# Layer-norm statistics of a transformer layer: three Newton steps from a bit-trick guess on VectorE, or a power on GpSimd and one Newton step

## The reference

```python
def _layernorm(x, eps=1e-05):
    m = jnp.mean(x, axis=-1, keepdims=True)
    v = jnp.var(x, axis=-1, keepdims=True)
    return (x - m) / jnp.sqrt(v + eps)

# attention, 16 heads of 16 features
q, k = features(split(x @ Wq + bq)), features(split(x @ Wk + bk))
#   features(y) = exp(y - max(y)) / (sum(exp(y - max(y))) + 1e-6)
probs = einsum('bhld,bhmd->bhlm', q, k) / (sum(q) + 1e-6)
x = _layernorm(x + merge(probs @ v) @ Wo + bo)

# feed-forward network, every operand through fp4_quant_dequant
#   scale = max(|block of 16|) / 6; round x / scale to a grid of 8 magnitudes
h = silu(fp4_linear(x, w_gate)) * fp4_linear(x, w_up)     # width 704
x = _layernorm(x + fp4_linear(h, w_down))
```

## Time and profile before

| what | value |
|---|---|
| time, median of 3 runs | 815.86 us (815.85 to 816.23) |
| time of the profiled execution | 815.38 us |
| its span | 813.6 us |
| TensorE busy | 734.0 us (90%) |
| VectorE busy | 747.7 us (92%) |
| ScalarE busy | 580.8 us (71%) |
| GpSimd busy | 573.3 us (70%) |
| mean granted TensorE clock | 0.981 of full speed |

### The profile page before, as it was taken

The page is one execution under the profiler, slowest core; times in us unless marked ns, Lnnn a source line. Parts: engine busy times, 40 slices in busy tenths (PEclk is TensorE's granted clock), DMA queues, the critical chain, the costliest instruction groups (busy, mean ns, idle before and its releaser), DMA issues.

```text
span 813.6 us, 20080 instructions
## 1 busy us (share of the span) xinstructions
PE 734.0 (90%) x4964; PEld 686.9 (84%) x4964; DVE 747.7 (92%) x1906; ACT 580.8 (71%) x1547; POOL 573.3 (70%) x613
## 2 busy tenths in 40 slices
PE   4999999999999968599899999999999999999994
PEld 3898888888888857599899899899899889889983
DVE  5999999999999998889999999999999999998883
ACT  3577777777777767477677777767767677768666
POOL 4676666666666655678778778778778878788762
PEclk9999999999999978899999999999999999999998
DMA  4122222212222110000000000000000000000002
GB/s 135 53 75 77 61 69 59 70 58 71 61 75 64 46 34 2 1 1 1 8 21 14 21 19 13 19 19 14 18 19 19 13 19 19 19 13 21 21 20 73
DMA packets 39718, 29.21 MB, mean 36 GB/s; under 512 B 3446, under 2 KB 39676, under 8 KB 39676
## 3 DMA queue, kind: packets, MB, share of 16 engines
q1 hardware_dynamic: 37228, 26.50, 10.6%
q10 hardware_dynamic: 2448, 2.23, 0.9%
HBM read 20.32 MB, written 8.39 MB: 35 GB/s over the span
## 4 chain that ended last, share of the span: by engine, by line
DVE 39%; PE 27%; issue 24%; DVEq 4%; POOL 3%; ACT 2%; DMA 0%; POOLq 0%; ACTq 0%; SPq 0%
PE bank L851 23%; DVE ln_t L624 3%; DVE ln_u L626 3%; DVE scratch L839 3%; DVE scratch L686 3%; DVE scratch L826 2%; DVE scratch L673 2%; DVEq L51 2%; DVE scratch L810 2%; DVE rounded L646 2%; DVE res L652 2%; PE wide L954 2%; DVE scratch L781 1%; DVE scratch L695 1%; DVE rstd L628 1%
## 5 line engine op out<-in xcount | busy, mean ns | idle before, releaser
L851 PE MATMUL bank<-wf_hi,rounded 128*128 128x352 f32 (+1 forms) x1792 | 409.8, 311 | 36.1 <-DVE rounded L832 21.6
L851 PEld LDWEIGHTS bank<-wf_hi,rounded 128*128 128x128 f32 x1792 | 301.8, 190 | 48.6 <-DVE rounded L832 28.3
L851 PE MATMUL bank<-wf_lo,rounded 128*128 128x352 f32 (+1 forms) x896 | 274.2, 306 | 0.0
L851 PEld LDWEIGHTS bank<-wf_lo,rounded 128*128 128x128 f32 x896 | 170.7, 191 | 0.0
L406 POOL TENSOR_TENSOR scratch<-scratch 128x704 f32<-128x704 f32 x64 | 95.8, 1497 | 97.8 <-DVE scratch L806 97.8
L851 PE MATMUL bank<-qkv_hi,rounded 128*128 128x512 f32 (+1 forms) x512 | 145.8, 339 | 0.0
L348 POOL TENSOR_TENSOR scratch<-scratch 128x512 f32<-128x512 f32 x64 | 67.9, 1061 | 75.8 <-DVE scratch L707 75.8
L390 POOL TENSOR_TENSOR scratch<-scratch 128x704 bf16<-128x704 f32 x64 | 100.4, 1569 | 1.8 <-ACT scratch L579 1.8
L851 PEld LDWEIGHTS bank<-qkv_hi,rounded 128*128 128x128 f32 x512 | 93.3, 191 | 9.9
L413 POOL TENSOR_TENSOR scratch<-scratch 128x704 f32<-128x704 bf16 x64 | 88.8, 1388 | 5.8 <-DVE scratch L810 0.7
L572 ACT ACTIVATE scratch<-scratch 128x704 uint8<-128x704 f32 x64 | 50.6, 791 | 52.8 <-POOL scratch L406 52.6
(11 more groups left out here) (102 smaller groups left out, 1771.6 us busy)
## 6 DMA issues: line engine op xcount, KB each, us to landing
scratch<-x_feat SPq DMA_DIRECT2D x64, 128.0 KB, 2.3
scratch<-x_tok SPq DMA_DIRECT2D x64, 128.0 KB, 2.0
out<-scratch SPq DMA_DIRECT2D x64, 128.0 KB, 1.7
scratch<-w_ffn ACTq DMA_DIRECT2D x17, 128.0 KB, 2.4
scratch<-L_attn_Wq SPq DMA_DIRECT2D x1, 256.0 KB, 2.7
scratch<-L_attn_Wk SPq DMA_DIRECT2D x1, 256.0 KB, 2.9
scratch<-L_attn_Wv SPq DMA_DIRECT2D x1, 256.0 KB, 3.7
wo<-L_attn_Wo SPq DMA_DIRECT2D x1, 256.0 KB, 3.2
```

The costliest lines, as they stand in the source:

```text
L851: last = pe.matmul(dst, x(c), w(c), start=first and n == 0, stop=n == len(terms) - 1)
```

## The change

The first guess becomes a power, (variance + epsilon) to the -1/2, in two operations on GpSimd: an addition of a constant tile that makes `ln_v`, and the power that makes `ln_y`. They stand at the end of GpSimd's step t = 0 in attention and of step t = 2 in the feed-forward part. VectorE keeps one Newton step and `nbias`, four operations in a row: in attention at the end of step 1, behind the masked copy, and in the feed-forward part at the end of step 3, between the reduce and the low part for which TensorE waits. The factor 1/D moves into ScalarE's scales (the square root of 1/D on each operand of the square), and `nbias` takes it back out. No other work is changed, and no other operation is moved.

```diff
-NEWTON = 3
-LN_OPS = 4 + 3 * NEWTON
+LN_OPS = 4
@@ GpSimd
+            pool.memset(ln_eps[:, :], LN_EPS)
+            pool.memset(ln_half[:, :], -0.5)
...
+            def first_guess(seq, norm, done, sq, guess):
+                stat = bass.ds(seq * T + norm * NT, T)
+                need(pool, done, seq * LN_OPS)
+                if norm == 1 and isinstance(seq, int) and seq == 0:
+                    pool.wait_ge(a_ln, NS * LN_OPS)
+                need(pool, sq, T * (seq + 1))
+                pool.tensor_tensor(ln_v[:, :], row_sq[:, stat], ln_eps[:, :], ALU.add).then_inc(guess, 1)
+                need(pool, guess, 2 * seq + 1)
+                pool.tensor_tensor(ln_y[:, :], ln_v[:, :], ln_half[:, :], ALU.pow).then_inc(guess, 1)
...
+                    if t == 0 and live_seq(i, -3):
+                        first_guess(i - 3, 0, a_ln, a_sq, a_guess)
...
+                    if t == 2 and live_seq(i, -2):
+                        first_guess(i - 2, 1, y_ln, y_sq, y_guess)
@@ ScalarE
-                act.activation(row_nm[:, at], row_sum[:, at], ACT.Copy, scale=-1.0 / D).then_inc(nm, 1)
+                act.activation(row_nm[:, at], row_sum[:, at], ACT.Copy, scale=-ROOT / D).then_inc(nm, 1)
...
                act.activation(dump[:, 1, :], res[:, rows(n)], ACT.Square, bias=row_nm[:, at],
-                               accum_out=row_sq[:, at]).then_inc(sq, 1)
+                               scale=ROOT, accum_out=row_sq[:, at]).then_inc(sq, 1)
@@ VectorE
-            def layer_norm(k, seq, norm, done, sq):
+            def layer_norm(seq, norm, done, guess):
...
+                if norm == 1 and isinstance(seq, int) and seq == 0:
+                    dve.wait_ge(a_x1, NT)
+                need(dve, guess, 2 * seq + 2)
+                dve.scalar_tensor_tensor(ln_t[:, :], ln_y[:, :], -0.5, ln_y[:, :], ALU.mult, ALU.mult).then_inc(done, 1)
+                dve.wait_ge(done, seq * LN_OPS + 1)
+                dve.tensor_tensor(ln_u[:, :], ln_t[:, :], ln_v[:, :], ALU.mult).then_inc(done, 1)
+                dve.wait_ge(done, seq * LN_OPS + 2)
+                dve.scalar_tensor_tensor(y, ln_u[:, :], 1.5, ln_y[:, :], ALU.add, ALU.mult).then_inc(done, 1)
+                dve.wait_ge(done, seq * LN_OPS + 3)
+                dve.scalar_tensor_tensor(nbias[:, at], row_nm[:, stat], 1.0 / ROOT, y,
+                                         ALU.mult, ALU.mult).then_inc(done, 1)
...
-                    ln(5)
+                    if t == 1 and live_seq(i, -3):
+                        layer_norm(i - 3, 0, a_ln, a_guess)
...
-                    ln(5)
+                    if t == 3 and live_seq(i, -2):
+                        layer_norm(i - 2, 1, y_ln, y_guess)
```

More of the change, by code:

```diff
@@ L67, in layer_kernel @@
     XB = D // BLK
+    ROOT = float(D) ** -0.5
     with ExitStack() as ctx:
@@ L82, in layer_kernel @@
         nbias = sb("nbias", [P, NT])
[L83 to L86, removed]
+        ln_v, ln_y, ln_t, ln_u = (sb(f"ln_{k}", [P, T]) for k in "vytu")
+        ln_eps, ln_half = (sb(f"ln_{k}", [P, T]) for k in ("eps", "half"))
         ident = sb("ident", [P, P])
@@ L202, in layer_kernel @@
             sem(f"a_{k}") for k in "xhi xlo xbo qk qkv max sub exp v sum eps rec feat".split())
-        a_post, a_qhi, a_qlo, a_kvm, a_c, a_chi, a_clo, a_out, a_res, a_sm, a_nm, a_sq, a_ln, a_x1 = (
-            sem(f"a_{k}") for k in "post qhi qlo kvm c chi clo out res sm nm sq ln x1".split())
+        a_post, a_qhi, a_qlo, a_kvm, a_c, a_chi, a_clo, a_out, a_res, a_sm, a_nm, a_sq, a_guess, a_ln, a_x1 = (
+            sem(f"a_{k}") for k in "post qhi qlo kvm c chi clo out res sm nm sq guess ln x1".split())
         e_max, e_s2s, e_invs, e_scs, e_xns, e_ys, e_mgs, e_cs, e_gs, x_q = (
@@ L210, in layer_kernel @@
             "gua gub sia sib ha hb hmax hs2 hinv hsc hxn hy hmg hc hg hq".split())
-        h_t, h_hi, h_lo, d_s, y_s, y_sm, y_nm, y_sq, y_ln, y_o = (
-            sem(f"b_{k}") for k in "ht hhi hlo d y ysm ynm ysq yln yo".split())
+        h_t, h_hi, h_lo, d_s, y_s, y_sm, y_nm, y_sq, y_guess, y_ln, y_o = (
+            sem(f"b_{k}") for k in "ht hhi hlo d y ysm ynm ysq yguess yln yo".split())
         block = ctx.enter_context(nc.Block())
@@ L605, in layer_norm @@
                 y = rstd[:, at]
[L606 to L628, removed]
-                op.then_inc(done, 1)
+                if norm == 1 and isinstance(seq, int) and seq == 0:
[9 more added lines that the diff above has]
+                                         ALU.mult, ALU.mult).then_inc(done, 1)
             def attention(i, steps=range(T)):
@@ L634, in attention @@
                     b, b1 = t % 2, (t - 1) % 2
-                    def ln(k):
-                        if t < 2 and live_seq(i, -3):
-                            k += 7 * t
-                            if k < LN_OPS:
-                                layer_norm(k, i - 3, 0, a_ln, a_sq)
                     def q_lo():
@@ L658, in attention @@
                         residual()
-                    ln(0)
                     if t == 3 and live_seq(i, 1, NW):
@@ L690, in attention @@
                         q_lo()
-                    ln(2)
-                    ln(3)
                     if live(i, t, -1):
@@ L702, in attention @@
                                           ALU.subtract).then_inc(a_sub, 1)
-                    ln(4)
                     if live(i, t, -1):
@@ L746, in ffn @@
                     even, odd = t % 2 == 0, t % 2 == 1
-                    def ln(k):
-                        if t >= 2 and live_seq(i, -2):
-                            k += 7 if t == 3 else 0
-                            if k < LN_OPS:
-                                layer_norm(k, i - 2, 1, y_ln, y_sq)
                     if even and live(i, t, 6):
```

8 lines of the change are left out of this document (removed).

## The result

The changed kernel takes **889.9 us** (median, 888.48 to 892.52) against 816.05 for the kernel before on the same chip: a ratio of 1.0906, interval 1.0879 to 1.0933. I had said slower, 828 us; it is slower by 74 us, six times what I had summed, and outside my range.

A forecast was written before the change was run, and what follows sets the result against it. Attention was taken as bound by VectorE, feed-forward by TensorE with VectorE close behind. Terms +8.4 + 7.8 - 3 - 0.9 = +12.3 on 815.38 gave 827.7, made 828 us; range 800 to 850, the forecast's own 817 to 840.

The forecast's parts named there:

- Chain and holds: Four dependent VectorE operations held by GpSimd's: 3.0 us in attention; in feed-forward step 3 the low part 4.05 us late.
- Rival A: Both loops: the chain slips between GpSimd operations and none is held; 775 us, spread over 765 to 805, chance 0.18.
- a TensorE clock that falls in the 3 us stalls: Feed-forward stalls: named within a rival as giving the same size as a dear power, 850 us; chance 0.08 for both.
- attention: Attention loop: period 18.8 us against 18.07, upper end 19.2; twelve calls give +8.4 us.
- feed-forward: Feed-forward loop: TensorE stalls 3.0 us, period 30.6 us against 29.96; twelve periods give +7.8 us.
- dear power: GpSimd's power: taken as 0.5 us, 0.2 us passed on in feed-forward; rival of 2 us or more, 850 us, chance 0.08.
- join, end and all else: Three first norms in the join lose nine operations each, -3 us; the last norm, alone, -0.9 us.
- The busy time of layer norms would hardly fall: VectorE: its busy time for layer norms was to hardly fall although 288 instructions went.

The follow-up runs named there:

- Experiment 5: The change with each of the four VectorE operations in the row made a reciprocal of one SBUF input, places and dependence kept; 790.95 us, 0.969 of the kernel before.
- experiments 6 and 7: The spread kernel with the row of four kept in attention alone (842.2 us), or in the feed-forward part alone (844.55 us).
- the spread kernel: The change with its four VectorE operations placed singly in attention step 1 and feed-forward step 3, power still on GpSimd; 796.0 us.
- exp. 8: The change with TensorE's two waits filled by 18 and 34 matmuls whose results are overwritten; 855.55 us, 1.0484 of the kernel before.
- Experiment 2: The change with a multiplication in place of GpSimd's power; 872.9 us, 1.072 of the kernel before.
- experiment 1: The run that made the spread kernel: the change with its four VectorE operations placed singly; 796.0 us, 0.9764 of the kernel before.
- experiment 10: The change without Newton step: GpSimd's power goes straight to the scale, GpSimd also makes the bias, VectorE keeps nothing; 785.2 us, 0.9627 of the kernel before.
- experiment 9: The spread kernel with the feed-forward four in a row at the end of the next call's step 0, ScalarE's normalisation moved to its step's end; 823.2 us.

## Why the prediction was right in kind and wrong in size

**Chain and holds: right.** Four held operations in attention, one free and three held in the feed-forward part, 2.9 and 3.96 us against my 3.0 and 4.05. Experiment 5 shows that a row that isn't held costs next to nothing, experiments 6 and 7 that the rows explain the whole distance to the spread kernel. The rule that I took from the Trainium skill ("SBUF — State Buffer", section "Who interferes with whom"), that a VectorE instruction with two inputs in SBUF contends with a GpSimd instruction that reads SBUF, agrees with the change's four operations, all of which are held in attention. It must not be read as "one input passes": the reciprocals of experiment 5 do, the one-input TENSOR_SCALARs shown there are held. That the number of inputs alone decides it for the four is not shown.

**Rival A: wrong as a rival, right as a price.** The chain didn't slip through. But its range for an unheld chain, 765 to 805 us, holds the three kernels that have no held row: 785, 791 and 796. The 156 ns of dispatch that the Trainium skill states for a VectorE instruction ("GPSIMD Engine Reference", section "Elementwise — side-by-side cycle accounting"), and that I weighed there, are close to the 0.15 to 0.18 us of the free operations in the rows above, and say nothing of the held ones.

**The term that failed: what a wait of TensorE costs.** I wrote "the same size would come from a TensorE clock that falls in the 3 us stalls; stalls of 1.04 us leave it at 1.00", and gave it a part of 0.08. I had extrapolated from a wait of 1 us to one of 3, and put the clock at nothing in the likeliest case. The trace of the kernel before even had a row that spoke for it, which I overlooked. Between the two loops TensorE waits 7.43 us, and works behind it at half clock:

```profile
342.23 0.66 PE L851 MATMUL bank<-wf_hi,rounded 128*128 128x352 f32 x1 [7.43 <-DVE wf_lo L720]
```

```profile
342.00:344.00 2.00, 1.77 (x6) 1.77 (x7) 1.97 (x8) 0.00 (x0) 0.00 (x0) 0.50 0.00 0
```

By periods (12 in each loop, from the first to the thirteenth of the 16 rows of the layer norm's first operation):

| term | predicted | measured | what it is made of |
|---|---|---|---|
| attention | +8.4 | +25.9 (216.73 to 242.66) | 18.8 forecast; 19.1 with holds alone (exp. 8), 20.45 with the clock |
| feed-forward | +7.8 | +48.1 (359.4 to 407.5) | 30.6 forecast; 31.86 with holds and dear power (exp. 8), 34.14 with the clock |
| join, end and all else | -3.9 | -1.3 (span +72.7 less the two) | not taken apart |

In attention the holds were mis-sized by 0.3 us (19.1 was in my upper end of 19.2), and the clock brought 1.35. In the feed-forward part the clock brought 2.28 of the 3.54 us that I missed. The remaining 1.26 is mostly the dear power: 1.02 us where I took 0.5, and passed on where I passed on 0.2. Experiment 2 shows how much: with the cheap guess TensorE's wait is 3.30 us, 0.85 less than the 4.15 of the change and near my 3.0. The other 0.4 us are not taken apart; no run has both the filled waits and the cheap guess. Of the 62 us between my 828 and the 890 measured, the clock is thus 39 (experiment 8, over 12 periods of each kind).

**"The busy time of layer norms would hardly fall": wrong in its words.** It fell from 171 us for 416 instructions to 91 us for 128. But VectorE's total fell from 747.7 to 727.8, only 20 us for 288 instructions. In part other operations take the holds that layer-norm operations took before: L770 and L774 last 1.86 and 0.60 us behind the power, and 0.68 and 0.18 in step 1; all operations but the layer norm's are 26 us longer in sum. The rest of the difference is overlap: in the record the short operations run in part at the same time as their neighbours, so that removing them frees less than their sum.

**What the change is worth without its row.** 815.7 to 796.0 us in experiment 1, and 815.9 to 785.2 in experiment 10, which leaves out the Newton step. The call without layer norms had set the most that could be won in attention at 1.6 us a period: the spread kernel won 1.57 (18.07 to 16.5).

## What to carry to other kernels

A few tiny dependent two-input operations on VectorE cost up to one GpSimd operation each if they stand in a row beside a busy GpSimd. Placed singly the same four cost 94 us less here, though in the feed-forward part three of them are still held: a hold costs little where VectorE would have waited anyway, which is my reading and not tested by itself. When a forecast contains a wait of TensorE longer than those whose clock was read, what the clock does behind it is an unknown with a price of its own: here keeping it up was worth 34 us of 74. Look for the trace's own longest waits and read the clock behind them first. An idle gap that a trace shows is not a place that stays idle once something is moved into it or away from what made it.

## What the runs showed of the hardware

- GpSimd takes 1.02 us for a power of 128x4 numbers and 0.20 us for a multiplication or addition of the same size (experiment 2 and the change).
- TensorE's granted clock fell from 1.00 to 0.50 (2.4 to 1.2 GHz) behind waits of 1.75, 2.31 and 4.15 us, and stayed at 1.00 behind waits of 0.94, 1.91 and 2.42 us; behind ten waits of 2.6 us in one loop it fell seven times (experiment 9). The length of the wait alone doesn't decide it. It is back at 1.00 3.5 to 5 us after the work has begun again. Filling the waits with matmuls of no use kept it at 1.00, and made the kernel faster.
- Four reciprocals of one SBUF input each pass beside a running GpSimd operation at 0.16 to 0.18 us; two-input operations of the same size, in the same place, take 0.50 to 0.96. A TENSOR_SCALAR with one input is held beside GpSimd's 704-column operation: 1.49 us on 128x4 (kernel before), 1.08 us on 128x32 (experiment 5).
